# A graph network kernel: the dense stage ahead of "gatv2" in pairs of groups, its tables written by ScalarE and scattered by GpSimd group by group

## The reference, cut to what matters

```python
h = unnL(X0)                                   # gather by edge_src, scale, segment_sum by edge_dst
X1 = -re_norm * h + X0 * (re_norm - 1.0)
h = unnL(X1)
Xi = -2.0 * re_norm * h + X1 * (2.0 * (re_norm - 1.0)) - X0
hc = jax.nn.relu(jnp.concatenate([X0, X1, Xi], axis=1) @ cheb_W + cheb_b)
fsrc = hc @ src_W + src_b
fdst = hc @ dst_W + dst_b
e = jax.nn.leaky_relu(fsrc[edge_src] + fdst[edge_dst], 0.2)
...
out = jax.ops.segment_sum(fsrc[edge_src] * a[:, :, None], edge_dst, num_segments=N)
```

## Time and profile before

| | us |
|---|---|
| median of 3 runs | 2537.11 (2536.48 to 2537.2) |
| profiled execution | 2538.81 |
| its span, first to last instruction | 2537.1 |
| mean granted TensorE clock | 0.882 of full |
| dense stage and what follows up to step 0 of "gatv2", in the span | 1112 to 1206 |

### The profile page before, as it was taken

How to read it: one execution, slowest core, us unless ns; L and a number is a source line. 1 busy time by engine, 2 the same in 40 slices (tenths; PEclk the granted TensorE clock), 3 DMA queues, 4 the chain that set the end, 5 groups by cost and what they waited for, 6 DMA issues and landing times.

```text
span 2537.1 us, 51142 instructions
## 1 busy us (share of the span) xinstructions
PE 1942.4 (77%) x20449; PEld 1701.2 (67%) x20449; DVE 1836.8 (72%) x4471; ACT 899.3 (35%) x906; POOL 1704.3 (67%) x1620
## 2 busy tenths in 40 slices
PE   2778777369994799966889946787788878589990
PEld 2777777259994799956888932455455545589990
DVE  7699998356554465534999863788887887699976
ACT  1377776334543245522444524000000000144542
POOL 6777775347775677756567751777777776567773
PEclk7888888579997899967999965899999999799995
DMA  6233333212221222213222215122211111332221
GB/s 231 69 114 113 114 120 110 76 39 75 67 73 45 52 74 67 67 23 141 80 61 57 61 31 238 49 50 50 50 49 50 50 50 41 134 87 67 68 62 21
DMA packets 83508, 194.79 MB, mean 77 GB/s; under 512 B 30864, under 2 KB 49624, under 8 KB 79554
## 3 DMA queue, kind: packets, MB, share of 16 engines
q1 hardware_dynamic: 31650, 139.14, 15.2%
q0 software_dynamic: 51744, 54.17, 11.6%
HBM read 107.89 MB, written 85.32 MB: 76 GB/s over the span
## 4 chain that ended last, share of the span: by engine, by line
PE 28%; POOL 25%; DVE 24%; issue 13%; ACT 6%; DMA 4%; ACTq 0%; POOLq 0%; DVEq 0%; SPq 0%
PE ps L763 25%; POOL edges_d L648 18%; DVE edges_d L1479 5%; POOL rows L648 3%; DVE rows L1207 3%; DVE edges_d L1406 3%; ACT scan L1015 3%; POOL agg L648 2%; DVE edges_d L1542 2%; PE ps L933 2%; POOL starts_dram L651 2%; DVE bigT L1479 1%; ACT edges_d L1000 1%; DVE agg L1173 1%; DMA starts_dram<-scan 1%
## 5 line engine op out<-in xcount | busy, mean ns | idle before, releaser
L648 POOL DMA_INDIRECT edges_d<-tab_y_dram,attr x425 | 433.9, 1021 | 183.5 <-issue 129.2
L763 PE MATMUL ps<-nodes,edges_d 125*128 125x160 bf16 x7140 | 498.4, 234 | 60.5 <-DVE nodes L1448 39.1
L763 PEld LDWEIGHTS ps<-nodes,edges_d 125*128 125x128 bf16 x7140 | 498.1, 98 | 61.1 <-DVE nodes L1448 39.5
L763 PE MATMUL ps<-nodes,aggn 125*128 125x180 bf16 (+2 forms) x3546 | 394.3, 244 | 117.5 <-DVE rows L1207 60.2
L648 POOL DMA_INDIRECT rows<-tab_cheb_dram,src_i x374 | 382.0, 1022 | 148.8 <-issue 113.3
L833 PE MATMUL ps<-edges_d,scan 125*125 125x480 bf16 x1700 | 364.8, 372 | 106.4 <-DVE edges_d L1947 106.4
L1207 DVE COPY_PREDICATED rows<-picks,ps 125x192 f32<-125x192 uint16 (+4 forms) x880 | 352.4, 402 | 122.1 <-PE ps L763 98.6
L833 PEld LDWEIGHTS ps<-edges_d,scan 125*125 125x125 bf16 x1700 | 228.3, 137 | 243.9 <-DVE edges_d L1947 110.7
L763 PE MATMUL ps<-nodes,agg 125*128 125x180 bf16 (+2 forms) x3564 | 339.1, 245 | 61.6 <-DVE rows L1207 61.1
L763 PEld LDWEIGHTS ps<-nodes,aggn 125*128 125x128 bf16 x3546 | 291.8, 101 | 124.0 <-issue 63.5
L763 PEld LDWEIGHTS ps<-nodes,agg 125*128 125x128 bf16 x3564 | 286.3, 101 | 67.3 <-DVE rows L1207 54.9
(11 more groups left out here) (362 smaller groups left out, 3109.1 us busy)
## 6 DMA issues: line engine op xcount, KB each, us to landing
src<-srcT_dram SPq DMA_DIRECT2D x70, 437.5 KB
scan_dram<-scan SPq DMA_DIRECT2D x17, 1700.0 KB
scan_dram<-scan SPq DMA_DIRECT2D x34, 425.0 KB
tab_y_dram<-edges_d SPq DMA_DIRECT2D x5, 2880.0 KB, 8.2
scanD_dram<-scan SPq DMA_DIRECT2D x34, 400.0 KB
starts_dram<-scan SPq DMA_DIRECT2D x2, 3400.0 KB, 13.9
edges_d<-tab_y_dram,attr POOLq DMA_INDIRECT x425, 2.6
src<-srcT_dram SPq DMA_DIRECT2D x18, 375.0 KB
```

The lines of the kernel that those rows point to most:

```text
L648: pool.indirect_dma_start(o, None, table, bass.IndirectOffsetOnAxis(index, 0)).then_inc(s, SLOT)
L763: ins = pe.matmul(column_ps(name, i), hots_[b][lot][:, i * NP:i * NP + P], parts_[:, part, at:at + PICKS * w], start=(lot == 0 and part == 0),
```

## The change

The order of the dense stage is written out in a list, DENSE_ORDER: groups 0, 1 and 2 one after another, then groups 3 and 4 with their steps alternating, then 5 and 6 likewise. TensorE and ScalarE follow it, and TensorE waits for the copy of the step whose result it reads instead of for all copies. ScalarE copies the second product in two instructions into `scat` and `tab`, where it was one into `aggn`. VectorE's two copies go, and a small memset signals to SyncE. GpSimd waits for the copy of each group and scatters that group's columns.

```diff
--- before.py
+++ after.py
@@ -112,6 +112,8 @@
         [("transpose", 3), ("transpose", 4), ("gates", 3), ("gates", 4)] + \
         [("transpose", 5), ("transpose", 6), ("gates", 5), ("gates", 6)]
     assert last == 6
+    DENSE_ORDER = [(what, g) for gs in ((0,), (1,), (2,), (3, 4), (5, 6))
+                   for what in ("transpose", "recurrence", "ends") for g in gs]
     MID = N // 2
     assert MID <= 2048
     BANK = 512
@@ -696,8 +698,11 @@
                     pool.wait_ge(table_stored, tables.up(SLOT))
                     run_pass(name)
 
-                pool.wait_ge(vec_for_sync, 5)
-                scatter_starts(starts32_dram, D)
+                for i, (what, g) in enumerate(DENSE_ORDER):
+                    if what == "ends":
+                        pool.wait_ge(group_copied, 3 * len(GROUPS) + i + 1)
+                        for j in GROUPS[g]:
+                            scatter(starts32_dram, start_i[:, j:j + 1], scat[:, j, 0:D], E - 1)
                 pool.wait_ge(table_stored, tables.up(2 * SLOT))
                 gather(first_row[:, 0:D], tab_fdst_dram, first_i[:, 0:1], first_in)
                 run_pass("gatv2")
@@ -906,18 +911,23 @@
                 mend("cheb1")
 
 
-                for tiles in GROUPS:
-                    pe.wait_ge(block_ready, J // LS + tiles[-1] // LS + 1)
-                    in_groups(lambda bank, a, j: pe.transpose(bank[0:3 * D, a * NP:(a + 1) * NP],
-                                                              aggn[:, j, 0:3 * D], ident[0:NP, 0:NP]), [tiles])
-                    all_copied()
-                    in_groups(lambda bank, a, j: pe.matmul(bank[0:D, a * NP:(a + 1) * NP], w_cheb[:, :],
-                                                           bigT[0:3 * D + 1, j * NP:(j + 1) * NP],
-                                                           start=True, stop=True), [tiles])
-                    all_copied()
-                    in_groups(lambda bank, a, j: pe.matmul(bank[0:NP, a * 2 * D:(a + 1) * 2 * D],
-                                                           tile_T(smallT, j)[0:D + 1, :], w_sd[:, :],
-                                                           start=True, stop=True), [tiles])
+                place = {step_: group.n + i + 1 for i, step_ in enumerate(DENSE_ORDER)}
+                for what, g in DENSE_ORDER:
+                    tiles = GROUPS[g]
+                    if what == "transpose":
+                        pe.wait_ge(block_ready, J // LS + tiles[-1] // LS + 1)
+                        in_groups(lambda bank, a, j: pe.transpose(bank[0:3 * D, a * NP:(a + 1) * NP],
+                                                                  aggn[:, j, 0:3 * D], ident[0:NP, 0:NP]), [tiles])
+                    elif what == "recurrence":
+                        pe.wait_ge(group_copied, place["transpose", g])
+                        in_groups(lambda bank, a, j: pe.matmul(bank[0:D, a * NP:(a + 1) * NP], w_cheb[:, :],
+                                                               bigT[0:3 * D + 1, j * NP:(j + 1) * NP],
+                                                               start=True, stop=True), [tiles])
+                    else:
+                        pe.wait_ge(group_copied, place["recurrence", g])
+                        in_groups(lambda bank, a, j: pe.matmul(bank[0:NP, a * 2 * D:(a + 1) * 2 * D],
+                                                               tile_T(smallT, j)[0:D + 1, :], w_sd[:, :],
+                                                               start=True, stop=True), [tiles])
                 mend("gatv2")
 
                 transposed = {}
@@ -1079,14 +1089,22 @@
                 first_hots("cheb1")
                 sum_pass("cheb1")
 
-                for group_ in GROUPS:
-                    copy_groups(lambda tiles: bigT[0:3 * D, columns(tiles)], lambda bank, n: bank[0:3 * D, 0:n * NP],
-                                groups=[group_])
-                    copy_groups(lambda tiles: smallT[0:D, columns(tiles)], lambda bank, n: bank[0:D, 0:n * NP],
-                                ACT.Relu, [group_])
-                    copy_groups(lambda tiles: aggn[:, tiles[0]:tiles[-1] + 1, 0:2 * D],
-                                lambda bank, n: bank[0:NP, 0:n * 2 * D].rearrange("p (j c) -> p j c", j=n),
-                                groups=[group_])
+                for what, g in DENSE_ORDER:
+                    group_ = GROUPS[g]
+                    if what == "transpose":
+                        copy_groups(lambda tiles: bigT[0:3 * D, columns(tiles)],
+                                    lambda bank, n: bank[0:3 * D, 0:n * NP], groups=[group_])
+                    elif what == "recurrence":
+                        copy_groups(lambda tiles: smallT[0:D, columns(tiles)], lambda bank, n: bank[0:D, 0:n * NP],
+                                    ACT.Relu, [group_])
+                    else:
+                        made_ = ps[0:NP, group.n % 2, 0:len(group_) * 2 * D].rearrange("p (j c) -> p j c", c=2 * D)
+                        js = slice(group_[0], group_[-1] + 1)
+                        act.wait_ge(group_in_psum, group.up())
+                        nc.scalar.activation(scat[0:NP, js, :], made_[:, :, D:2 * D], ACT.Copy)
+                        nc.scalar.activation(tab[:, :, :].rearrange("p j c -> p (j c)")[0:NP, 0:J * D]
+                                             .rearrange("p (j c) -> p j c", c=D)[:, js, :], made_[:, :, 0:D], ACT.Copy)\
+                            .then_inc(group_copied, 1)
                 softmax_pass("gatv2")
 
 
@@ -1832,8 +1850,7 @@
                                              ALU.mult, ALU.add).then_inc(block_ready, 1)
                 vec.wait_ge(group_copied, group_n.up(3 * len(GROUPS)))
 
-                vec.tensor_copy(tabD, aggn[:, :, 0:D]).then_inc(vec_for_sync, 1)
-                vec.tensor_copy(scat[0:NP, :, :], aggn[:, :, D:2 * D]).then_inc(vec_for_sync, 1)
+                vec.memset(idle[:, 0:1], 0.0).then_inc(vec_for_sync, 2)
                 begin_pass("gatv2", tabD, 5)
 
                 vec.tensor_copy(att_ps, att1[:, :]).then_inc(vec_done, 1)
```

## The result

| | before | after |
|---|---|---|
| median on one chip | 2537.15 us (2536.48 to 2539.14, 4 runs) | 2522.91 us (2521.14 to 2524.61, 4 runs) |
| profiled execution | 2538.81 us | 2524.61 us |
| its span | 2537.1 us | 2522.9 us |
| mean granted clock | 0.882 | 0.885 |

The ratio of the comparison is 0.9939, with a 95% interval of 0.9927 to 0.9951; the quotient of the two medians, 0.9944, lies in it. Their difference is 14.2 us, as forecast, and so is that of the two profiled executions.

What follows compares the result with a forecast made beforehand. GpSimd's scatter path ended 8.57 us after TensorE's and VectorE's. With scatters earlier and the dense stage shortened, VectorE goes on at 1181.0 instead of 1195.17: 2537.11 - 14.2 = 2522.9 us, range 2517.5 to 2526.5.

Steps and rivals of the forecast that it cites:

- The scatters start earlier: GpSimd after its last cheb1 gather: 25 scatters from 1134.97, 33.6 us in all, edges in at 1175.3, 19.9 us earlier.
- The dense stage in pairs: Groups 3 with 4 and 5 with 6 on TensorE: 9.4 and 6.7 us, second products ending at 1147.1.
- the gates' 3.62: Measured row used for the pairs: first layer's gates, 16 matmuls of two groups in one piece, 3.62 us.
- ScalarE writes the tables: End of dense stage: stage ends 1147.5, 4.7 us earlier; VectorE gains 6.4, one-hots start 5.6 us earlier.
- The other path: TensorE and VectorE, one-hots to the edges' copy: VectorE ready at 1181.0 instead of 1195.17, now last, 14.2 us gained.
- The end that had 2 us for this: Range term for TensorE's lead: up to 2 us longer or shorter at the lower clock.
- Through the pass: Chunks of the gatv2 pass: GpSimd's and TensorE's queues are timed from VectorE, so all 14.2 us reach the end.
- the scatters stay last: Rival, 8 in 100: dearer scatters keep GpSimd's path last; 2534.1 us if all cost what the first did.
- the gain is spent in the pass: Rival, 4 in 100: some gatv2 queue has slack of its own, the pass ends where it does now, 2537.
- The half clock of the lead: Rival, 4 in 100: TensorE's lead stays at 1.2 GHz, VectorE goes on 9.9 us later than before, 2547.0.
- the rising clock: Rival, 15 in 100: TensorE's clock rises inside the paired dense stage, VectorE ready at 1176, gain 19, 2518.1 us.
- The 0.92 for "faster": Whole kernel: chance given to a faster result, from forecast, rising clock and most of the late scatters.

Runs made afterwards that it cites:

- after_again: The kernel after, unchanged, run once more in the second set on another chip; median 2523.67 us, ratio 0.9935 to the kernel before.
- after_third: The kernel after, unchanged, run a third time on another chip; median 2537.96 us, ratio 0.9944 to the kernel before.
- delay18: The kernel after with 18 small memsets on GpSimd ahead of its first scatter; median 2530.89 us, ratio 0.9959 to the kernel before.
- late_scatter: The kernel after, but GpSimd waits for the copies of all groups before its first scatter; median 2530.74 us, ratio 0.9963 to the kernel before.
- early_src: The kernel after with SyncE's source loads of the lead and chunk 0 issued ahead of the table stores; ratio 0.9931 to the kernel before.
- early_lead7: The kernel after with early source loads and a gatv2 lead of 7 columns instead of 11; 2534.77 us, ratio 0.9926 to the kernel before.
- the third set: Last four runs, on one chip: the kernel before with a lead of 7 columns (ratio 1.0003), early_src, early_lead7 and after_third.

## Why the prediction was right, step by step

**The scatters start earlier.** Forecast first at 1134.97, last at 1167.6; measured 1135.53 and 1167.20. The last gather itself came 0.55 later in this execution, the gap of 0.30 is as forecast. The row of 25 takes 32.65 us to the end of the last (1167.20 + 0.98 - 1135.53) instead of 33.6: near the lower end of 32. The first scatter takes 1.02 instead of 1.72, as supposed of one without VectorE's copies beside it. The slack is 6.9 instead of 5.7. The first twelve scatters took until 1151.07, 15.5 us, so the last group's copy at 1147.74 was well ahead of its turn. No later wait held anything: from first to last there is nothing but the gap of issue.

**The dense stage in pairs.** Forecast from 1130.99 to 1147.5, 16.5 us with ScalarE's two copies; measured from 1131.87 to 1147.74 (by the chain), 15.9. The terms written down for groups 5 and 6 add up to 6.9 and not to the 6.7 that went into the sum; measured are 6.8, from 1140.65 to 1147.41. The phases of 3.47 and 3.54 us for 16 products are what the gates' 3.62 promised, and the two copies of 128 columns took 0.28 and 0.27 with 0.18 between their starts, 0.45 together, against 0.34 from the gates' half as wide ones.

**ScalarE writes the tables.** VectorE's cast at 1147.96 for 1147.7, first one-hot at 1153.71 for 1153.3 with 1.85 us of waiting for the source load; from the last gather it is 19.43 for 19.6. The load was issued at 1148.86 instead of 1148.5, behind two stores. The forecast gave the one-hots 5.6 us of gain, with 5.1 and 6.1 as ends: it is 5.8 by the landmark.

**The other path.** Forecast 1181.0, measured 1181.78; by the landmark 47.3 and 47.50. The lead was 0.5 us longer than before (26.17 from first one-hot to the last take, against 25.65): TensorE's clock was granted in full later, as the stretches 1160 to 1166 at 0.65 and 1163 to 1166 at 0.79 say, against 3.5 us at 0.51. The end that had 2 us for this took it in. The second half of chunk 0 was covered: the take at 1188.68 follows without a wait.

**Through the pass.** By the landmarks 13.94 are gained at the copy and 12.74 at the store behind the pass, 1.20 less; 0.55 were lost ahead of the last gather, and 2.01 gained in what comes behind the pass, 1.67 of it in the spline stage. So the sum agrees to the tenth by chance: its parts are right to about a microsecond. The 1.20 is no steady price of the pass: from "edges" to "store" the same program took 333.83 in after_again and 333.31 in after_third, the kernel before 333.84, the kernel after 335.04 in its first profile. The waits of GpSimd in this pass, by line, show where its lead over VectorE goes (columns as in the earlier trace rows):

```profile
POOL rows L650 <- DVE bigT L1560: 41.6, 10, 15.4
```

Ten waits as before, the longest 6.6 us longer: about the 6.9 us of slack, spent waiting for VectorE's row buffers.

**The rivals.** That the scatters stay last is refuted by the row at 1181.78, that the gain is spent in the pass by the 333 to 336 us. The half clock of the lead did not come: it ran at 1.00 from 1166. The one that was given too little is the rising clock, 15 in 100: it came in 6 of the 10 profiled executions with pairs, and in none of the 4 without. Its size was right for the execution in which the rise lasted longest: forecast were VectorE ready at 1176 and a gain of 19, and after_again has 42.39 after the gather, which is 1176.1 on the clock of before, and 19.05. In after_third, where the clock fell back sooner, the gain is 16.5. The step that failed in it is the weighing of rows: the stage's own row at 0.50 was busy for 7.85 of 10 us only, and the spline's, busy throughout, is of another shape. The Trainium skill, TensorE: Matmul & The Clock Gate, "Part 1: The HAM clock gate", says that activity releases the throttle; after_again agrees, and the first profile of the same program, busy for 10.00 of 10 us at 0.50, does not. The ratios of the kernel after, 0.9939, 0.9935 and 0.9944, are 15.5, 16.5 and 14.2 us of 2537, between the forecast and this rival or at the forecast; in how many of the other executions the clock rose is not known. The 0.92 for "faster" is more than its parts give, 68, 15 and at most 8 in 100.

## What to carry to other kernels

Where two paths meet, read the idle row ahead of the meeting point: its 8.57 us said what the first one could give before the other would have to be shortened too, and here the early scatters with ScalarE's tables brought 9 by the landmark, pairs and tables without them 6 to 8, and the whole 14. Start a long row of issues when its first input is there and not its last, if its engine is idle: here that was worth 7 us on top of the tables. A deliberate delay of a known length then shows what slack is left, if the wait that it causes is read from the trace and not from the total time. Compare executions from a landmark just ahead of the change to one just behind it; an untouched stage can vary by more than the effect.

## What the runs showed of the hardware that was not expected

The granted clock of one and the same program rose within the dense stage in one execution and not in another: 0.92 over 1134 to 1142 in after_again, 0.50 over 1131 to 1141 in the first profile. In all six executions that had it, the rise came at the same place, 0.6 to 0.8 us behind the start of the last gather. They differ in how long it lasted: in after_again the clock was at 1.00 until 7.5 us behind the gather, in after_third, delay18, late_scatter, early_src and early_lead7 only until 4.0, and then at 0.50 again. Over the 10 us behind the gather that is a mean of 0.84 and of 0.67. The stretches of after_third:

```profile
1130.00:1134.00 4.00, 4.00 (x19) 3.25 (x19) 0.44 (x2) 1.61 (x4) 3.08 (x4) 0.50 0.10 16
1134.00:1139.00 5.00, 4.60 (x35) 3.70 (x33) 1.03 (x3) 2.79 (x8) 3.78 (x5) 0.84 0.06 13
1139.00:1144.00 5.00, 3.94 (x18) 3.18 (x16) 0.23 (x2) 1.44 (x6) 3.78 (x5) 0.50 0.05 11
```

Within its second stretch the clock was at 1.00 from 1134 to 1137, with TensorE busy for 2.99 of 3 us, and at 0.70 over 1137 to 1138, busy for 0.96 of 1: it fell while TensorE had work. Neither the rise nor the fall follows from what TensorE did in these rows, and no run here shows the cause. The rise was seen with pairs alone, 6 of 10 against 0 of 4; that the pairs cause it is likely, and with four executions on one side not shown.

The spline stage, which no edit touches, took 640.56 us before and 636.77 to 658.17 in the others. In the third set, on whose chip the kernel before had 2551.8 us instead of 2539.27, all four lie above 652. So part of it belongs to the chip; the rest of the spread is unexplained.
